# One half of a broadcast moved from SyncE's DMA queue to ScalarE's in six of sixteen batches of a decoder block

## The reference

```python
x = layernorm(x + attn(x))                      # 16 batches of 128 x 128, 16 heads of width 8, rope
x = layernorm(x + xattn(x, ctx, ctx))           # correlation by FFT, top 11 lags, softmax over them, roll of v
x = layernorm(x + moe(x))                       # 8 experts of width 256, the 2 best of each row
...
qkv = einsum('bsd,ed->bse', x, w_qkv)
q, k = apply_rope(q), apply_rope(k)
attn = softmax(einsum('bhsd,bhtd->bhst', q, k) * HD**-0.5, axis=-1)
out = einsum('bhst,bhtd->bhsd', attn, v)
out = einsum('bsd,ed->bse', out, w_out) + b_out
```

## Time and profile before

| what | value |
| --- | --- |
| median of three runs | 231.52 us (231.08, 231.52, 233.53) |
| the profiled execution, its own time | 231.02 us |
| its span, first to last instruction | 229.2 us |
| granted TensorE clock over the span | 0.994 |
| busy: PE, PEld | 214.5 us (94%), 184.1 us (80%) |
| busy: DVE, ACT, POOL | 180.9 us (79%), 142.5 us (62%), 111.2 us (49%) |
| the chain that ended last: PE, DMA, DVE, ACT | 79%, 7%, 6%, 3% |

### The profile page before, as it was taken

One profiled execution on the slowest core, in us unless ns is written; L12 is line 12 of the kernel. 1 busy time (PEld: TensorE's weight loads), 2 busy tenths in 40 slices (PEclk: granted clock), 3 DMA queues, 4 the chain that ended last, 5 costly groups with the idle time before them and its releaser, 6 DMA issues.

```text
span 229.2 us, 7213 instructions
## 1 busy us (share of the span) xinstructions
PE 214.5 (94%) x2724; PEld 184.1 (80%) x2724; DVE 180.9 (79%) x622; ACT 142.5 (62%) x248; POOL 111.2 (49%) x219
## 2 busy tenths in 40 slices
PE   7989899999999979999999999999999999999970
PEld 7766677787777667778887999789988999889970
DVE  0588999999899899876755779897798868875885
ACT  2487899999999995674489300991029610596112
POOL 5189879999989995513630400252002600040484
PEclk9999999999999999999999999999999999999997
DMA  5951634665655651420000000001000100001001
GB/s 138 286 134 35 106 59 65 158 135 106 149 122 91 43 92 18 127 74 1 3 0 0 3 0 1 0 4 45 4 0 0 46 3 1 0 4 46 1 16 34
DMA packets 32454, 12.32 MB, mean 54 GB/s; under 512 B 19906, under 2 KB 32290, under 8 KB 32418
## 3 DMA queue, kind: packets, MB, share of 16 engines
q1 hardware_dynamic: 31554, 11.48, 24.1%
q10 hardware_dynamic: 864, 0.36, 0.7%
HBM read 6.33 MB, written 1.05 MB: 32 GB/s over the span
## 4 chain that ended last, share of the span: by engine, by line
PE 79%; DMA 7%; DVE 6%; ACT 3%; issue 2%; SPq 1%; DVEq 0%; ACTq 0%
PE bank L1328 13%; PE scoreT_pair L1328 12%; PE score_pair L1298 11%; PE scoreT_pair L1298 8%; PE bank L1042 6%; PE bank L1046 5%; PE bank L965 4%; PE scoreT_pair L997 4%; PE score_pair L981 3%; DMA qT_all<-mT 2%; PE bank L1003 2%; PE bank L1059 2%; DMA early<-in_ctxT 2%; DMA qT_all<-stack 2%; PE scoreT_pair L945 2%
## 5 line engine op out<-in xcount | busy, mean ns | idle before, releaser
L1385 DVE TENSOR_REDUCE rowmax<-score_pair 128x8 f32<-128x1024 f32 x32 | 39.0, 1218 | 4.4 <-PE score_pair L981 3.5
L608 POOL TENSOR_TENSOR ve<-mv,table 128x4 f32<-128x4 f32 (+1 forms) x12 | 3.3, 275 | 78.1 <-DVE mv L1745 60.2
L737 ACT ACTIVATE early<-scoreT_pair 128x1024 f32<-128x1024 f32 x32 | 32.8, 1026 | 6.3 <-PE scoreT_pair L997 6.1
L1328 PE MATMUL bank<-w,early 128*128 128x128 f32 x256 | 30.1, 276 | 0.0
L1328 PE MATMUL scoreT_pair<-w,early 128*128 128x128 f32 x256 | 29.9, 275 | 0.0
L1328 PEld LDWEIGHTS bank<-w,early 128*128 128x128 f32 x256 | 29.5, 192 | 0.3
L1328 PEld LDWEIGHTS scoreT_pair<-w,early 128*128 128x128 f32 x256 | 29.2, 192 | 0.0
L1298 PE MATMUL score_pair<-x2T_part,w_part 128*128 128x512 f32 x108 | 28.4, 398 | 0.0
L880 ACT ACTIVATE early<-score_pair,b 128x512 f32<-128x512 f32 x38 | 25.9, 690 | 3.2 <-PE score_pair L1298 2.6
L1042 PE MATMUL bank<-early,v_pad 128*32 128x128 f32 x512 | 26.5, 279 | 0.4 <-DVE attnT L1401 0.3
L1046 PE MATMUL bank<-early,head_ones 128*32 128x128 f32 x512 | 25.8, 273 | 0.0
(11 more groups left out here) (229 smaller groups left out, 472.3 us busy)
## 6 DMA issues: line engine op xcount, KB each, us to landing
w<-in_w SPq DMA_DIRECT2D x8, 256.0 KB, 3.7
x_ext<-in_x SPq DMA_DIRECT2D x4, 256.0 KB, 5.6
qT_all<-mT SPq DMA_DIRECT2D x32, 32.0 KB, 2.3
early<-in_xT SPq DMA_DIRECT2D x3, 256.0 KB, 4.8
early<-in_ctxT SPq DMA_DIRECT2D x3, 256.0 KB, 5.4
out<-qkv_all SPq DMA_DIRECT2D x3, 256.0 KB, 2.3
table<-in_tables SPq DMA_DIRECT2D x1, 321.0 KB
qT_all<-stack SPq DMA_TRANSPOSE x13, 3.3
```

What stands on the lines that cost most here:

```text
L737: act.activation(prob[n % 2][:, 2 * u:2 * u + 2, :, :], scoreT_pair[:, :].rearrange("p (i j s) -> p i j s", i=2, j=QUAD), ACT.Exp, scale=S ...
L1328: mm = pe.matmul(expert_bank[k % 4][:, e4 * D:(e4 + 1) * D], hT[:, f, n * P:(n + 1) * P], w2[:, f, :], start=(c == 0), stop=(c == CH - 1))
L1385: dve.tensor_reduce(rowmax[:, H // 2 * u:H // 2 * (u + 1)], score_pair[:, :].rearrange("p (r t) -> p r t", t=S), AX_X, ALU.max).then_inc(s ...
```

## The change

In batches 0, 1, 12, 13, 14 and 15 SP issues only the first of the two DMAs of the spread. ScalarE issues the second one itself, after a wait for `m_T`, at a place of its list that is a little behind `mT_copy(n)` in batches 0, 1 and 12, and directly behind it in batches 13, 14 and 15. The data, their place and the semaphore counts are the same.

```diff
+        TWO_QUEUES = (0, 1, 12, 13, 14, 15)
+        def spread_half(eng, n, at):
+            rows = slice(at, at + H)
+            eng.dma_start(qT[n % DEEP][rows, :, :], mT[n % 2][rows, :].unsqueeze(1).broadcast_to([H, H // 2, S]))\
+                .then_inc(s_m[n % DEEP], 16)
...
                 sp.wait_ge(s["m_T"], n + 1)
-                for at in (MROW, SLOT + MROW):
-                    rows = slice(at, at + H)
-                    sp.dma_start(qT[n % DEEP][rows, :, :], mT[n % 2][rows, :].unsqueeze(1).broadcast_to([H, H // 2, S]))\
-                        .then_inc(s_m[n % DEEP], 16)
+                spread_half(sp, n, MROW)
+                if n not in TWO_QUEUES:
+                    spread_half(sp, n, SLOT + MROW)
...
+            def spread_other_half(n):
+                act.wait_ge(s["m_T"], n + 1)
+                spread_half(act, n, SLOT + MROW)
...
             mT_copy(0)
             keep_qkv(5)
+            spread_other_half(0)
             kT_copy(2)
...
             mT_copy(1)
             second_piece(4)
+            spread_other_half(1)
             second_copy(4)
             softmax_exp(0, 1)
...
             mT_copy(12)
             second_piece(15)
+            spread_other_half(12)
             kT_copy(14)
...
             mT_copy(13)
+            spread_other_half(13)
             softmax_exp(12, 0)
...
             mT_copy(14)
+            spread_other_half(14)
             softmax_exp(13, 0)
             softmax_exp(13, 1)
             mT_copy(15)
+            spread_other_half(15)
             softmax_exp(14, 0)
```

## The result

The changed kernel takes 235.15 us (median of five runs, 234.62 to 236.45) against 231.52 before: ratio 1.0146, 95% interval 1.0093 to 1.0199. It is slower by 3.6 us in the medians, and by 3.94 us in the profiled executions (234.96 against 231.02, spans 233.2 and 229.2).

The account below looks back on a forecast made before the run. TensorE bounds 28 to 73 us, ScalarE has no room from 73.0 to 83.5; early gain -0.66 plus late loss 2.15 makes +1.49, on 231.3 giving 232.8 us, range 230.2 to 235.1.

Parts of the forecast that it names:

- dear issue: Rival: each ScalarE issue costs 1.02 us, SP's slowest; net +3.6 us, 234.9 us; chance 0.14.
- Batches 0 and 1: Early spreads: TensorE's waits of 0.32 and 0.80 us shrink or vanish, `scoresT(1, 0)` starts 0.66 us earlier.
- cover of `keep_qkv(5)`: Batch 0: ScalarE's 0.60 us issue runs beside it; any excess is taken up by 0.53 us idle time.
- strict reading of the Trainium skill: Batch 1: a second issuer saves only one issue, 0.64 us, and the half lands at about 27.7.
- Through the bound stretch these 0.66 us are kept: From 28 to 73 us TensorE is the bound, so the early gain of 0.66 us carries through unchanged.
- The issue costs 0.59 to 0.60, and what stands behind it waits: ScalarE's DMA issue: price 0.59 to 0.60 us, bounds 0.50 and 1.02; the instruction behind it starts only afterwards.
- terms of 12: Late delays: batch 12 `kT_copy(14)` +0.47 us; 14 exponential +0.58, TensorE 0.52 later; 15 +0.58.
- term of 13: Uncovered issue between `mT_copy(13)` and `softmax_exp(12, 0)`: adds about 0.58 to the 0.47 us, 1.05 later together.
- free issue: Rival: the issue costs ScalarE nothing, late loss gone, early gain 1.12 us; 230.2 us; chance 0.18.
- missing early gain: Rival: batch 1's half still lands late or another wait follows; only 2.15 us loss, 233.4 us; chance 0.15.
- SP's side: SP loses one issue in each of six batches; earlier turns of q and w2 load gain nothing.

Follow-up runs that it names:

- e9_later1: Only batches 0 and 1 split, batch 1's issue moved behind `second_copy(4)`, against the kernel before: 231.66 us against 231.70, ratio 0.9991.
- e1_early: Only batches 0 and 1 split over two queues, against the kernel before: 231.29 us against 231.44, ratio 0.9979.
- e10_no12: Batches 0, 1, 13, 14, 15 split, the last three issued behind the exponential, against the kernel before: 230.55 us against 231.70, ratio 0.9947.
- e2_late: Only batches 12 to 15 split, against the kernel before: 235.04 us against 231.44, ratio 1.0140, four runs.
- e3_filled: Changed kernel plus six useless matmuls ahead of `scoresT(12, 1)`: 233.62 us against the changed kernel's 235.15; ratio to the kernel before 1.0102.
- e6_only13: Only batch 13 split, issue in front of the exponential, against the kernel before: 233.31 us against 231.57, ratio 1.0043.
- e4_covered: Changed kernel with ScalarE's issues of batches 13 to 15 moved behind the exponential: 231.64 us against 231.44 of the kernel before, ratio 1.0019.
- e5_wait_only: SP issues both halves everywhere, ScalarE keeps the six added waits without DMAs, against the kernel before: 231.65 us against 231.57, ratio 1.0020.
- e8_only12: Only batch 12 split, issue behind the second piece of 15, against the kernel before: 232.13 us against 231.57, ratio 1.0029.
- e7_14_15: Only batches 14 and 15 split, against the kernel before: 232.40 us against 231.57, ratio 1.0016.
- e11_13_filled: Only batch 13 split, plus four useless matmuls ahead of `scoresT(12, 1)`, against the kernel before: 232.56 us against 231.70, ratio 1.0038.

## Why the prediction was right, and where not

The sign was right, and so was the reason for it: issues on ScalarE ahead of the exponential cost more than the early ones gain. The size was not. The forecast was 1.49 us over before in the traces' terms, and the profiled executions differ by 3.94. The time, 235.15, lies at the very upper end of the range, where the prediction has its dear issue (234.9, and 235.1 with the spread of the runs). That issue didn't happen, so that the range holds the time is luck. The outcome, more than 1% slower, had a chance of 0.27.

**Batches 0 and 1** were right to 0.1 us: forecast 0.66, measured 0.74, or 0.67 without the head start of this execution. The steps by which it comes (the exponential at 24.75, `weighted(0, 1)` at 25.82) were right too. The cover of `keep_qkv(5)` was short by some 0.2 us, since the issue took 0.74 and not 0.60, and the idle time took it up, as the prediction had it for that case. The strict reading of the Trainium skill ("DMA: Bandwidth & Descriptors", "Issuing engines are not separate DMA queues"), by which only the issue time is saved, is not borne out in the first half of its consequence: the half landed near 26.2, 23.78 + 2.4, not near 27.7. `e9_later1`, where a half took 4.2 us on SP's queue, shows that the landing varies by more than the issue. The prediction puts the long landing down to the turn of q(4) on the same queue; no run moved that turn, so this stays an inference.

**"Through the bound stretch these 0.66 us are kept"** was wrong. I read from TensorE's 44.65 of 45.00 us that nothing else could bind. One landing of a turned q was 1.0 us longer than before and took 0.52. In `e1_early` 0.72 were kept, in `e10_no12` nothing. The kernel before has a slow turn there too, 4.9 us, just within its slack. That the earlier TensorE is what runs into it is not shown: near 47 to 54 us ScalarE waits for a turn of q in four of the six kernels with the early gain (0.31 to 0.59 us), and in five of the seven without it (0.21 to 0.45 us, `e2_late` 0.32). What the prediction had wrong is that nothing but TensorE's own work could bind there; how much is lost is scatter of the landing, as far as these traces tell.

**"The issue costs 0.59 to 0.60, and what stands behind it waits"** was right: 0.60 to 0.61 in the four late batches, and 0.10 us until the next start where I had 0.02 to 0.03. With it the terms of 12 (0.47, as forecast), 14 (0.68 for 0.58) and 15 (0.61 for 0.52, the slack taken off in both) are near. I had read the 0.05 us between the end of `mT_copy(13)` and the exponential as the copy holding the exponential; it was the scores that held it, as the run with the wait alone shows. The term of 13 was 0.97 for 0.58: behind the issue there is a further 0.33 us in ScalarE's queue before the exponential, as the chain that ended last shows for the changed kernel (start, us, what):

```profile
84.15 0.60 ACTq L269
84.75 0.33 issue
85.08 0.02 ACTq L85
```

It is there in the changed kernel and in `e3_filled`, and not in `e2_late` or `e6_only13`, where the exponential starts 0.10 to 0.11 us behind; its cause is open.

**The missing term is the clock**, 1.43 us of the 2.45 that the forecast falls short. The prediction let TensorE wait over a microsecond more ahead of `scoresT(12, 1)`, in front of the 0.52 us that were there before, and priced this as time lost only. It had the clock at 1.00 in its rows and did not ask what the new idle time does to it. `e3_filled` shows it: the same delay of ScalarE, 0.15 us of wait in place of 1.49, and the 1.43 us gone. The rest of the shortfall is 0.44 of early gain (0.52 lost on the way less 0.08 more at the start), 0.39 in batch 13, and 0.19 in batches 14 and 15.

**The rivals.** The free issue is refuted by the gaps, the missing early gain by 27.61 (0.67 came, though 0.52 were lost later), and the dear issue too, though its 234.9 comes closest to the measured 235.15: the issue was 0.60, not 1.02. That closeness is chance. SP's side gave nothing, as written.

## What to carry to other kernels

A DMA issued by a computing engine is a step of that engine's list with a price, here 0.60 us (the first one 0.73 to 0.75) and 0.1 more. In this kernel it was free behind the start of an exponential of 1.02 us that doesn't depend on it, and dear between a copy and the exponential for which TensorE waits. Before adding a wait of a microsecond or more to TensorE, ask what it does to the clock, which can double the bill: batch 13 alone cost 1.7 us in the medians, and 0.9 with the wait filled. And a saving at the start of a pipeline is only kept if each slower transfer behind it has the slack for it.

## What was not expected of the hardware

- The granted clock fell to 0.50 after waits of 1.49 and 0.52 us (the changed kernel), 1.20 and 0.52 (`e2_late`), and 1.19 and 0.52 (`e6_only13`). It did not after 0.15 and 0.52 (`e3_filled`), nor after 0.35 and 0.52 in `e4_covered`, `e5_wait_only` and `e8_only12`, nor after 0.70 and, four microseconds later, 0.79 in `e7_14_15`. In `e6_only13` it fell when only some 0.2 us of the second wait had passed. No run has the long wait without the second, so the part of the second is open.
- The clock stayed down for 3.4 us in the changed kernel and in `e2_late`, and for 6.8 in `e6_only13`, so nearly the same waits had two prices. One of the four executions of `e2_late` has 0.994 over its span, where the other three have 0.978 to 0.987, and is the fastest of them (233.91 us).
- ScalarE's first issue of the spread took 0.73 to 0.75 us in all eleven kernels that have one, wherever it stood, and each later one 0.59 to 0.62. Why is open.
- The same 32 KB spread landed between 2.1 and 4.4 us after its issue. In five of the kernels of the experiments (`e3_filled`, `e4_covered`, `e5_wait_only`, `e8_only12`, `e11_13_filled`) TensorE waited for one or both of the last two spreads (batches 14 and 15), 0.4 to 0.9 us in all; `e5_wait_only`, where SP issues all of them as before, had the longest, 0.89. The kernel before had no such wait of a matmul in its trace. This is scatter of the landing, and one reason why effects under 0.5% are hard to measure here.
